# Slots to tokens: rows loaded into the buffer they are summed in, sum and norm a step later, the turn between two halves of the scores

## The reference, cut to what matters

```
o = o + y.reshape(Bx, NS, D)
out = _mha(x, o, o, c_Wq, c_bq, c_Wk, c_bk, c_Wv, c_bv, c_Wo, c_bo)
...
x = _layernorm(x + _L0_ffn_ref(x, ...), axis=-1)
```

## Time and profile before

| | |
|---|---|
| median of 3 runs | 4001.34 us (3987.97 to 4004.26) |
| the profiled execution | 3993.84 us, its span 3992.2 us |
| the stage slots_to_tokens | from 3755 us of the span to its end |
| its loop, first scores to last mix | 3818.29 to 3976.96 us |
| mean granted TensorE clock | 0.958 of 2.4 GHz |
| busy over the whole span | PE 91%, DVE 55%, ACT 44%, POOL 47% |

### The profile page before, as it was taken

The page is one execution under the profiler, slowest core; times in us unless marked ns, Lnnn a source line. Parts: engine busy times, 40 slices in busy tenths (PEclk is TensorE's granted clock), DMA queues, the critical chain, the costliest instruction groups (busy, mean ns, idle before and its releaser), DMA issues. The chain is left out here.

```text
span 3992.2 us, 65646 instructions
## 1 busy us (share of the span) xinstructions
PE 3620.1 (91%) x19584; PEld 2250.6 (56%) x19584; DVE 2186.2 (55%) x5904; ACT 1751.5 (44%) x3767; POOL 1860.8 (47%) x1684
## 2 busy tenths in 40 slices
PE   6999999999999999998678999999899978788686
PEld 4777777777677777776334555555455532122253
DVE  4666656666566666666686667666333321111355
ACT  4666656666566666665234555555221210000033
POOL 3666656666566666665345777777311000000112
PEclk8999999999999999999898999999999988889898
DMA  7999999999899999999453222222354339999623
GB/s 274 387 387 382 380 351 385 382 382 386 333 385 392 381 382 385 388 381 340 160 186 110 84 90 87 83 85 72 124 186 150 111 135 414 417 418 416 256 90 121
DMA packets 412824, 1083.54 MB, mean 271 GB/s; under 512 B 24640, under 2 KB 90688, under 8 KB 363328
## 3 DMA queue, kind: packets, MB, share of 16 engines
q1 hardware_dynamic: 395312, 1031.95, 68.7%
q10 hardware_dynamic: 16656, 47.19, 3.0%
q0 software_dynamic: 512, 0.26, 0.0%
HBM read 642.58 MB, written 436.73 MB: 270 GB/s over the span
## 5 line engine op out<-in xcount | busy, mean ns | idle before, releaser
L553 POOL TENSOR_SCALAR a_sc<-a_sc,a_inv 128x512 f32<-128x512 f32 x512 | 822.6, 1607 | 584.1 <-DVE a_inv L496 539.0
L505 DVE COPY a_pt<-a_ps_t 128x512 f32<-128x512 f32 x512 | 353.4, 690 | 545.4 <-PE a_ps_t L237 528.0
L1099 POOL TENSOR_SCALAR b_sc<-b_sc,b_inv 128x128 f32<-128x128 f32 (+3 forms) x512 | 546.3, 1082 | 182.8 <-DVE b_inv L1068 179.4
L375 ACT ACTIVATE a_stage_q<-a_ps_b 128x640 f32<-128x640 f32 x512 | 360.5, 704 | 584.4 <-PE a_ps_b L255 552.2
L1029 ACT ACTIVATE b_sc<-b_sc,b_mx 128x128 f32<-128x128 f32 (+3 forms) x512 | 281.9, 552 | 320.6 <-DVE b_mx L1062 320.4
L365 ACT ACTIVATE a_sc<-a_sc,a_mx 128x512 f32<-128x512 f32 x512 | 370.0, 723 | 55.7 <-DVE a_mx L489 52.2
L489 DVE CUSTOM_DVE_ANT_0 a_sc<-a_ps_s,a_rq 128x512 f32<-128x512 f32 x512 | 353.1, 690 | 74.5 <-PE a_ps_s L227 59.7
L375 ACT ACTIVATE a_stage_k<-a_ps_b 128x640 f32<-128x640 f32 x512 | 357.7, 699 | 0.0
L237 PEld LDWEIGHTS a_ps_t<-a_ident,a_sc 128*128 128x128 f32 x2048 | 247.3, 141 | 146.1 <-issue 140.7
L1062 DVE CUSTOM_DVE_ANT_0 b_sc<-b_ps_s,b_mask 128x128 f32<-128x128 f32 (+3 forms) x512 | 229.3, 489 | 161.8 <-PE b_ps_s L977 157.9
L237 PE MATMUL a_ps_t<-a_ident,a_sc 128*128 128x128 f32 x2048 | 308.4, 273 | 8.8 <-DVE a_pt L505 8.8
(11 more groups left out here) (206 smaller groups left out, 6377.3 us busy)
## 6 DMA issues: line engine op xcount, KB each, us to landing
band_q<-a_stage_q SPq DMA_DIRECT2D x128, 1280.0 KB, 6.8
band_k<-a_stage_k SPq DMA_DIRECT2D x128, 1280.0 KB, 9.7
a_rk<-band_k SPq DMA_DIRECT2D x128, 1024.0 KB, 12.6
a_rq<-band_q SPq DMA_DIRECT2D x256, 512.0 KB, 13.5
d_w<-in_e_W SPq DMA_DIRECT2D x24, 4096.0 KB, 42.8
d_wg<-in_e_Wg SPq DMA_DIRECT2D x16, 4096.0 KB, 28.2
keep<-in_e_W SPq DMA_DIRECT2D x8, 4096.0 KB, 36.2
a_okv<-in_b_wkv ACTq DMA_DIRECT2D x62, 512.0 KB, 7.9
```

The source lines that it names most:

```text
L375: act.activation(st[h % 2][:, t, :], src, ACT.Copy).then_inc(sem[f"a_{kind}_staged"], 1)
L505: dve.tensor_copy(pt[:, h % 2, :, t * P:(t + 1) * P], ps_t[:, :].rearrange("p (r n) -> p r n", r=T4)).then_inc(sem["a_pt_out"], 1)
L553: pool.tensor_scalar(sc[n][:, :], sc[n][:, :], inv[:, n:n + 1], None, ALU.mult)\
L1099: pool.tensor_scalar(sc[j % 2][i][:, 0:width(i)], sc[j % 2][i][:, 0:width(i)], inv[j % 2][:, i:i + 1], None, ALU.mult).then_inc(sem["b_nor ...
```

## The change

In `slots_to_tokens` and the loads issued ahead of it:

- The rows x(b) are loaded into the h buffer in which they are summed and normalized; there are three h (and three statistics) buffers and no x buffers. GpSimd adds c_bo in place.
- x and xT have semaphores of their own. SyncE's step s is: xT(s+1) (waits for scores of s-1), store of s-2 (waits for its norm), x(s+1) (from batch 3 on waits until the store of batch s-2 has landed).
- VectorE's step s is: sum and statistics of s-2, first half of the softmax of s (to the subtraction), scale and shift of s-2, second half of the softmax of s.
- TensorE's step s is: scores of two token tiles of s, turn of s-1, scores of the other two, mix of s-1.
- ScalarE's step s is: copy of the turned probabilities (s-1), root (s-2), exponential (s), norm (s-2).
- All steps, now 0 to 9, are written out; there is no hardware loop.
- Ahead of the loop VectorE's memsets and the copies of bq come behind the copy of the transposed slots, and GpSimd waits for these transposes before its first addition.

```diff
-            sp.dma_start(x0, dr["x2"](0)).then_inc(sem["e_in0"], 16)
+            sp.dma_start(x0, dr["x2"](0)).then_inc(sem["e_x_in0"], 16)
...
-        x = [x0, sb("x1", [P, T4, E])]
-        h = [sb(f"h{i}", [P, T4, E]) for i in range(2)]
+        h = [x0, sb("h1", [P, T4, E]), sb("h2", [P, T4, E])]
...
-        st = [sb(f"st{i}", [P, T4, 16]) for i in range(2)]
+        st = [sb(f"st{i}", [P, T4, 16]) for i in range(3)]
...
-            def load(b, j):
-                if not early(b, 2):
+            def load_xT(b):
+                if b >= 2:
                     sp.wait_ge(sem["e_scored"], b - 1)
                     settle()
-                    sp.wait_ge(sem["e_xb"], b - 1)
+                sp.dma_start(xT[b % 2][:, :, :], dr["x2T"](b)).then_inc(sem[f"e_in{b % 2}"], 16)
+
+            def load_x(b):
+                if b >= 3:
+                    sp.wait_ge(sem[f"e_stored{b % 3}"], 16 * (b // 3))
                     settle()
-                sp.dma_start(xT[j][:, :, :], dr["x2T"](b)).then_inc(sem[f"e_in{j}"], 16)
-                sp.dma_start(x[j][:, :, :], dr["x2"](b)).then_inc(sem[f"e_in{j}"], 16)
-
-            def store(b, j):
+                sp.dma_start(h[b % 3][:, :, :], dr["x2"](b)).then_inc(sem[f"e_x_in{b % 3}"], 16)
+
+            def store(b):
                 sp.wait_ge(sem["e_normed"], b + 1)
                 settle()
-                sp.dma_start(dr["out"](b), h[j][:, :, :]).then_inc(sem[f"e_stored{j}"], 16)
-
-            def step(s, j):
-                if inside(s, -1, B):
-                    load(s + 1, 1 - j)
-                if inside(s, 1, B):
-                    store(s - 1, 1 - j)
-
-            for j in range(2):
-                sp.sem_inc(sem[f"e_stored{j}"], 16)
+                sp.dma_start(dr["out"](b), h[b % 3][:, :, :]).then_inc(sem[f"e_stored{b % 3}"], 16)
+
+            def step(s):
+                if s + 1 < B:
+                    load_xT(s + 1)
+                if s >= 2:
+                    store(s - 2)
+                if 1 <= s + 1 < B:
+                    load_x(s + 1)
+
             sp.dma_start(y[:, :], dr["y_all"]).then_inc(sem["e_const_in"], 16)
-            loop(sp, B, step, 1)
-            for j in range(2):
-                sp.wait_ge(sem[f"e_stored{j}"], 8 * B + 16)
-
+            steps(step)
+            for i in range(3):
+                sp.wait_ge(sem[f"e_stored{i}"], 16 * len(range(i, B, 3)))
...
-            def scores(b, j):
-                pe.wait_ge(sem[f"e_in{j}"], (b - j) * 16 + 32)
-                if not early(b, 1):
-                    pe.wait_ge(sem["e_biased"], b)
-                for t in range(T4):
+            def scores(b, half):
+                if half == 0:
+                    pe.wait_ge(sem[f"e_in{b % 2}"], 16 * (b // 2) + 16)
+                    if b:
+                        pe.wait_ge(sem["e_biased"], b)
+                for t in (2 * half, 2 * half + 1):
                     for k in range(K4):
-                        mm = pe.matmul(ps_s[:, t // 2, (t % 2) * HS:(t % 2 + 1) * HS], xT[j][:, k, t * P:(t + 1) * P],
+                        mm = pe.matmul(ps_s[:, t // 2, (t % 2) * HS:(t % 2 + 1) * HS], xT[b % 2][:, k, t * P:(t + 1) * P],
                                        a[:, k, b, :, :].rearrange("p m n -> p (m n)"),
                                        start=(k == 0), stop=(k == K4 - 1))
-                mm.then_inc(sem["e_scored"], 1)
-
-            def turn(b, j):
+                if half:
+                    mm.then_inc(sem["e_scored"], 1)
...
-            def step(s, j):
-                if inside(s, 0, B):
-                    scores(s, j)
-                if inside(s, 1, B):
-                    turn(s - 1, 1 - j)
-                    mix(s - 1, 1 - j)
+            def step(s):
+                if s < B:
+                    scores(s, 0)
+                if 0 <= s - 1 < B:
+                    turn(s - 1)
+                if s < B:
+                    scores(s, 1)
+                if 0 <= s - 1 < B:
+                    mix(s - 1)
...
-            dve.memset(kd[:, :, :, :, :].rearrange("p m b h s -> p (m b h s)"), 0.0).then_inc(sem["e_kd"], 1)
-            dve.memset(vd[:, :, :, :, :].rearrange("p m b h s -> p (m b h s)"), 0.0).then_inc(sem["e_kd"], 1)
             dve.memset(eps[:, :], EPS).then_inc(sem["e_eps"], 1)
             dve.wait_ge(sem["e_const_in"], const_in)
             dve.tensor_tensor(o[:, :], o[:, :], y[:, :], ALU.add).then_inc(sem["e_o"], 1)
             dve.wait_ge(sem["e_o"], 1)
             dve.tensor_tensor(o[:, :], o[:, :], b2[:, :], ALU.add).then_inc(sem["e_o"], 1)
+            dve.wait_ge(sem["e_oT_ready"], 1)
+            dve.tensor_copy(oT[:, :, :].rearrange("p k n -> p (k n)"), ps_t[:, 0, :]).then_inc(sem["e_oT"], 1)
+            dve.memset(kd[:, :, :, :, :].rearrange("p m b h s -> p (m b h s)"), 0.0).then_inc(sem["e_kd"], 1)
+            dve.memset(vd[:, :, :, :, :].rearrange("p m b h s -> p (m b h s)"), 0.0).then_inc(sem["e_kd"], 1)
             for m in range(K4):
                 dve.tensor_copy(bq[:, m, :], cols[:, 0, m:m + 1].to_broadcast([P, P])).then_inc(sem["e_bq"], 1)
-            dve.wait_ge(sem["e_oT_ready"], 1)
-            dve.tensor_copy(oT[:, :, :].rearrange("p k n -> p (k n)"), ps_t[:, 0, :]).then_inc(sem["e_oT"], 1)
...
-            def step(s, j):
-                if inside(s, 0, B):
-                    soft_in(s, j)
-                    soft_out(s, j)
-                if inside(s, 1, B):
-                    norm_in(s - 1, 1 - j)
-                    norm_scales(s - 1, 1 - j)
-                    norm_out(s - 1, 1 - j)
-
-            loop(dve, B, step, 1)
+            def step(s):
+                if s >= 2:
+                    norm_in(s - 2)
+                    norm_scales(s - 2)
+                if s < B:
+                    soft_in(s)
+                if s >= 2:
+                    norm_out(s - 2)
+                if s < B:
+                    soft_out(s)
+
+            steps(step)
 
         @block.gpsimd
         def _(pool):
-            def step(b, j):
-                pool.wait_ge(sem[f"e_in{j}"], (b - j) * 16 + 32)
-                pool.wait_ge(sem[f"e_stored{j}"], (b - j) * 8 + 16)
+            def add(b):
+
+                pool.wait_ge(sem[f"e_x_in{b % 3}"], 16 * (b // 3) + 16)
                 for t in range(T4):
-                    ins = pool.tensor_tensor(h[j][:, t, :], x[j][:, t, :], bo[:, :], ALU.add)
+                    ins = pool.tensor_tensor(h[b % 3][:, t, :], h[b % 3][:, t, :], bo[:, :], ALU.add)
                 ins.then_inc(sem["e_xb"], 1)
 
             pool.wait_ge(sem["e_const_in"], const_in)
-            loop(pool, B, step, 0)
+            pool.wait_ge(sem["e_oT_ready"], 1)
+            for b in range(B):
+                add(b)
 
         @block.scalar
         def _(act):
             fold_out(act, 1, lambda d, s: act.activation(d, s, ACT.Copy))
 
-            def step(s, j):
-                b, i = s - 1, 1 - j
-                if inside(s, 1, B):
-                    act.wait_ge(sem["e_turned"], b + 1)
-                    if not early(b, 1):
-                        act.wait_ge(sem["e_mixed"], b)
-                    act.activation(pt[:, :, :], ps_t[:, :, :], ACT.Copy).then_inc(sem["e_pt"], 1)
-                if inside(s, 0, B):
-                    act.wait_ge(sem["e_shifted"], s + 1)
-                    act.activation(sc[j][:, :, :], sc[j][:, :, :], ACT.Exp, scale=SCALE_F).then_inc(sem["e_exped"], 1)
-                if inside(s, 1, B):
-                    act.wait_ge(sem["e_var"], b + 1)
-                    act.activation(st[i][:, :, 8:9], st[i][:, :, 7:8], ACT.Sqrt, bias=eps[:, :])\
-                       .then_inc(sem["e_std"], 1)
-                    act.wait_ge(sem["e_scales"], b + 1)
-                    for t in range(T4):
-                        ins = act.activation(h[i][:, t, :], h[i][:, t, :], ACT.Identity, bias=st[i][:, t, 10:11],
-                                             scale=st[i][:, t, 9:10])
-                    ins.then_inc(sem["e_normed"], 1)
+            def std(b):
+                act.wait_ge(sem["e_var"], b + 1)
+                act.activation(st[b % 3][:, :, 8:9], st[b % 3][:, :, 7:8], ACT.Sqrt, bias=eps[:, :])\
+                   .then_inc(sem["e_std"], 1)
+
+            def turned_out(b):
+                act.wait_ge(sem["e_turned"], b + 1)
+                if b:
+                    act.wait_ge(sem["e_mixed"], b)
+                act.activation(pt[:, :, :], ps_t[:, :, :], ACT.Copy).then_inc(sem["e_pt"], 1)
+
+            def softexp(b):
+                act.wait_ge(sem["e_shifted"], b + 1)
+                act.activation(sc[b % 2][:, :, :], sc[b % 2][:, :, :], ACT.Exp, scale=SCALE_F).then_inc(sem["e_exped"], 1)
+
+            def norm(b):
+                act.wait_ge(sem["e_scales"], b + 1)
+                for t in range(T4):
+                    ins = act.activation(h[b % 3][:, t, :], h[b % 3][:, t, :], ACT.Identity, bias=st[b % 3][:, t, 10:11],
```

(57 more changed lines are left out.)

20 lines of the change are left out of this document (11 added, 9 removed).

## The result

The changed kernel takes 3957.11 us (median of 4 runs, 3955.31 to 3963.19) against 3994.65 of the kernel before; the ratio is 0.9911, 95% interval 0.9895 to 0.9926, so 30 to 42 us less; the medians lie 37.5 us apart. Forecast were 34.5 us less and 3965.

A forecast was written before the change was run, and what follows sets the result against it. Loads waiting behind SyncE's store were taken as the bound. Loop 30.5 plus start 4.0 made 34.5 us less: 3959.3 from the profiled run, 3966.8 from the median; set at 3965, range 3948 to 3986.

The forecast's parts named there:

- The step's floor: Loop: TensorE's mix, scores and turn back to back, 14.9 us, the least a new step can take.
- What bounds the kernel now: Loop before: no engine, but SyncE's loads, late behind the previous batch's store, which waits for its norm; 19.4 us a step.
- the second ring: Loop before: mix, sum, norm, next copy, next mix; the forecast noted only mixes 2.61 and 9.27 us behind the copy.
- A late mix delays probabilities: VectorE's queue: sum and statistics stand ahead of the next softmax; a resulting TensorE idle loses 1.6 us more a step.
- rival B: Loop: gain under 20 us, through VectorE's queue; steps of 17.0 to 17.7 us, 3979 to 3984 us; chance 0.13.
- First steps: Loop's beginning: TensorE idles 3.2 us before batch 0's turn, 1.6 added for the lower clock; the change loses 3.7 here.
- T(2): Start of the scores of batch 2, counted from those of batch 0: 28.4 us, before 24.7.
- rival A: Loop: floor missed by a late load or VectorE under GpSimd's lock; 15.4 to 16.1 us a step, 3970 to 3974; chance 0.20.
- SyncE's cover: Loop: the load of xT behind store and x lands 1.1 us before its scores want it, so it stays hidden.
- GpSimd beside VectorE: Loop: GpSimd's additions lengthen the softmax's multiply by up to 1.0 us a step, perhaps the subtract too; hidden by 2.4 spare.
- Step 8: Loop's last turn and mix: turn waits until 1.1 us, mix runs from 3.3 for 7.1 us.
- Start: Ahead of the loop: VectorE takes up the keys 4.0 us earlier by the reordering, range 1 to 5.

The follow-up runs named there:

- x6: Kernel before with ScalarE issuing the stores behind its norm, so SyncE's queue holds loads alone: stage 237.0 us against 236.7, ratio 1.0005.
- x7: Changed kernel with the old order of sum, statistics and norm on VectorE and ScalarE; buffers, separate loads and split scores stay: stage 236.5 us against 203.0, ratio 0.9995.
- x9: Changed kernel with x buffers and SyncE's old load order back, the norm still behind the next copy: stage 199.6 us against 203.0, ratio 0.9896.
- x10: x6 with ScalarE's root, norm and store also moved behind the copy of the next batch's turned probabilities: stage 216.4 us against 237.0, ratio 0.9963.
- x2: Changed kernel with the part ahead of the loop put back as before: stage 205.9 us against 203.0, ratio 0.9936.
- x4: Changed kernel without GpSimd's additions of c_bo, the signal kept: stage 197.2 us against 203.0, ratio 0.9903.
- x5: Changed kernel with SyncE issuing the load xT(s+2) ahead of the store of batch s-2: stage 200.0 us against 203.0, ratio 0.9915.

## Why the prediction was right, and where it was not

The total was right: 34.5 us forecast, 33.7 in the stage. That it came so close is in part luck: the loop gained 26.9 us of the 30.5 forecast, the start 6.3 instead of 4.0, with 2.6 by the clock that nothing in the forecast provided for, and the end behind the last mix 0.5 that was put at nothing. The terms:

- **The step's floor** of 14.9 us: measured 14.65, in the steps that nothing disturbed. Right.
- **What bounds the kernel now** was wrong as a diagnosis. "The wait that ends last in a step is the load's" took one turn of the chain for the whole: the load's ring was there, but it was one of two. I had the second ring's rows at hand (mixes waiting 2.61 and 9.27 us for the copy) and booked it as a small saving under ScalarE. x6 and x7 show that with the loads cured and the norm left where it was nothing is gained, x9 that the loads can stay as they were once the norm has moved, x10 and x7 that the norm's place gives and takes most of it. The sum held since it was not made from the removed wait but from the new schedule, engine by engine, in which neither ring was left.
- **"A late mix delays probabilities"**: rival B's ring through VectorE did not come; in the changed kernel VectorE is late by GpSimd, not by the mix.
- **First steps**: T(2) at 26.5, forecast 28.4. TensorE idled 2.98 us, but here the clock stayed up. Six steps took 90.2 us against 89.4, 15.0 each: rival A's sign, waits for xT, was seen, but not its 15.4 us a step.
- **SyncE's cover** of 1.1 us: overdrawn twice, by 0.28 and 1.02 us, by the path VectorE, norm, store, x, xT, as rival A had it; the transfers themselves took what was forecast (4.2 for the store, 7.6 for xT).
- **GpSimd beside VectorE**: mis-sized. I gave it at most 1.0 us on the multiply and perhaps 1.0 on the subtract; the four instructions of scale and shift, which I had as 0.6 us hidden under the exponential, took 2.3. At the last turn, where no cover is left, this came out: 3.21 us late instead of 1.1, and 0.9 + 1.6 us at the lower clock. Step 8 took 15.0 us, forecast 10.4. The Trainium skill ("SBUF — State Buffer", section "Who interferes with whom") says of a VectorE instruction with two SBUF inputs that it contends with a GpSimd one that reads SBUF, and that the order of issue and not the shape decides who blocks; the trace agrees, with 0.37 and 2.31 us for the same four.
- **Start**: 4.0 forecast, 3.65 by the reordering, in the range of 1 to 5, and 2.6 more by the clock, which x2 had without it. For bq the forecast kept 3.8 us beside GpSimd's additions, and it took 3.82; without them it took 0.56 (x4).
- **Split and new loads**: the forecast gave no term to either, only to the new schedule as a whole. The split is worth about nothing beside GpSimd's additions and 4 us without them.

Open: the 2.6 us of clock in the start; what either ring was worth alone in the kernel before; and how much of x9's 3.4 us under the changed kernel is more than the last turn's luck.

## What to carry to other kernels

Follow each ring to its end, not the chain of waits once: where two rings have nearly the same length, the chain passes from one to the other, and curing the one it names can give nothing. A step's in-order queue is part of the ring: ask of every instruction in it whom it keeps waiting, and move what nobody needs soon (here the norm) behind what the critical engine needs next (the copy). And price a new schedule by all its covers at its last step too, where nothing hides a late engine any more.

## What the hardware showed that was not expected

After idle times that are the same to 0.01 us TensorE's clock was found at either level. The turn after 2.98 or 2.99 us of idle took 1.09 us in the changed kernel, x2 and x5, and 1.97 us (granted clock 0.50, the lower level of 1.2 GHz) in x4, x7 and x9; x9's following scores took 5.65 us against 3.62. The 24 matmuls of the fold after 3.69 us took 13.19, 12.26 or 10.57, at granted clocks of 0.80, 0.86 and 1.00. In x6 the mixes after 3.42 us took 9.93, 7.13 and 8.83. By these pairs a forecast of one such stretch can be off by some 3 us, an estimate.

VectorE's smallest instructions can be its dearest: one element per partition, up to 1.23 us each beside GpSimd's additions, whose median is 1.27, against 0.15 alone. The copies of bq, each a column spread over 128x128, have one input only and still went from 0.56 us for all four (x4) to 3.82 beside these additions.
